# Gathers of a pairwise-product recommender kernel let go by a count of finished pieces

## The chip, the core and the metric

One core of one Trainium2 chip runs the whole program. The metric is the device time of one launch in microseconds. The five engines work in parallel: TensorE (PE in the rows; PEld is its weight load), VectorE (DVE), ScalarE (ACT), GpSimd (POOL) and SyncE (SP), ordered by semaphores that the kernel waits on.

## What is computed

A batch of 1024 rows looks up 32 embeddings of 64 numbers each in 32 tables. For each of the 496 pairs of fields (p, q) a 64x64 matrix multiplies one embedding and the result is multiplied with the other and summed; the 496 sums and 16 dense numbers go through three dense layers. All is float32.

```python
e = jnp.stack([tbl_0[ids[:, 0]], ..., tbl_31[ids[:, 31]]], axis=1)      # 1024 x 32 x 64
p = emb_inputs[:, ROW]
q = emb_inputs[:, COL]
kp = jnp.einsum('bpj,ipj->bpi', p, kernel)
outputs = jnp.sum(kp * q, axis=-1)                                       # 1024 x 496
...
h = jnp.concatenate([z, dense_ctx], axis=1)
h = jnp.maximum(h @ W_top1 + b_top1, 0.0)
h = jnp.maximum(h @ W_top2 + b_top2, 0.0)
y = h @ W_top3
```

## The kernel before

**Blocks and tiles.** The batch is cut into 4 blocks of 256 rows (`BLOCKS`, `SIZE`), the 32 fields into 16 tiles of two fields (`TILES`). Tile number m counts through all blocks: m = 16 b + tile (in block 0 the first five come in another order, `FRONT`). There are 64 (`LOOKED_UP`).

**Look-up of a tile (L369 to L383, GpSimd).** Four indirect gathers, one for each of two fields and two halves of 128 rows, each 128 rows of 64 numbers into `nat`, which has 8 places (`RING`); tiles 0 and 1 of a block go to `nat01`, which is doubled. They wait until tile m - 8 is transposed (L374), so that the place is free. Three tiles of block 0 (m = 0, 1, 3, `BY_PRODUCT`) are not gathered but looked up by a product with a one-hot matrix, so there are 61 look-ups, 244 gathers. The gathers of tile m count up `gathered[m % 8]`.

**Transposition.** TensorE transposes the gathered halves into `t_ps` (L586) and counts up `transposed`; ScalarE copies them to `rows` (L454) and counts up `rows_ready`. From block 1 on two tiles are transposed at a time.

**Pieces.** A piece is what VectorE multiplies in one instruction, 128x1024. There are two kinds. A *double* (48 a block) takes two pairs of tiles: TensorE multiplies `k_sb` with `rows` into one of three buffers of `u_ps` (L629, 8 matmuls; L636, 16 matmuls, for the two pieces of a block that pair the fields within tiles, multiplied by `by_self`), VectorE multiplies by `rows` (L549, or L552) into `prod`, and TensorE later adds up over the 64 partitions with `sel` into `z_ps` (L663, L669), four pieces behind. A *pass* (14 a block) has the batch on the partitions (L650, 8 matmuls), VectorE multiplies by `nat01` (L560), and ScalarE sums along the row with 16 pairs of small instructions (L466). So a block has 62 pieces, the kernel 248. TensorE may run three pieces ahead of VectorE (`URING`). Each product counts up `prod_ready`.

**Order.** A piece needs all tiles up to its own, so work opens up tile by tile: of a block, nothing but 7 pieces can be done without tiles 6 and up. `Plan` writes out one order of pieces for all engines by a small model of time: when a tile has landed (`landed`, with `issued`, `there`), it lets TensorE put its transposition behind every fourth double (`behind`) if it is there 1.5 us before, and before a piece (`before`) when nothing else is left. Every engine walks through that order.

**The sync queue (SP)** loads `k_sb` in 14 parts (the later ones behind `transposed`, L424), the swapped copies `by_self` (L411, behind `rows_ready`), and the weights of the towers.

**Ends.** Before the first piece TensorE and VectorE do the one-hot look-ups; behind the last piece come the three dense layers (L710, L730, L738).

Of the kernel before, what the change touches and what calls it, by code (L numbers as in the profile page):

```python
# [9 lines left out]
TILES = FIELDS // 2  # L10
# [3 lines left out]
SUBS = SIZE // P  # L14
# [18 lines left out]
ND = len(DOUBLES)  # L33
# [4 lines left out]
NP = len(IN_PASSES) // 2 * SUBS  # L38
# [35 lines left out]
URING, PRING, CRING, RING, LANES = 3, 8, 3, 8, 8  # L74
# [27 lines left out]
def tile_at(m):  # L102
    b, tile = divmod(m, TILES)
    return b, FRONT[tile] if b == 0 and tile < len(FRONT) else tile
# [11 lines left out]
def lane_count(m):  # L116

    return 32 * SUBS * (m // LANES + (m % LANES not in BY_PRODUCT))

K_FIRST = [min(d for d, double in enumerate(K_ORDER) if (double[1] or double)[0] == tile) for tile in range(2, TILES)] + [NK]
K_AFTER_TILE = [max(0, tile - 3) for tile in range(2, TILES)]

START, GATHER, LANDING = 3.2, 1.25, 2.35
PIECE, QUAD, TURN, TRANSPOSE, COPY, FOLD, FILL, PRODUCT, COMPARE = 0.87, 0.87, 0.17, 0.33, 0.55, 0.5, 0.23, 3.5, 3.2


class Plan:
# [7 lines left out]
    def __init__(self):  # L137
        self.order, self.before, self.behind, self.quads, self.sums, self.folded = [], [], [], [], [], []
        self.fill = [0] * LOOKED_UP
        self.now, self.copied, self.issued, self.there, self.done, self.here = 5.6, 0, START, [], [], []  # L140
        self.open, self.passes, self.summed, self.folds, self.doubles = [], 0, [], 0, 0
        while self.doubles < BLOCKS * ND:
            self.step()
        while self.open:
            self.add_sums(SUMS, 0)

    def landed(self, m):
        while len(self.there) <= m:
            n = len(self.there)
            if n in BY_PRODUCT:  # L150
                self.there.append(0)
                continue
            self.issued = max(self.issued, self.done[n - RING] if n >= RING else 0) + 2 * SUBS * GATHER
            self.there.append(self.issued - GATHER + LANDING)
        return self.there[m]

# [46 lines left out]
    def append(self, what):  # L203
        self.order.append(what)
        self.before.append(self.here)
        self.here = []
        self.behind.append([])
        self.quads.append(range(0))
        self.sums.append([])
        self.folded.append(None)  # L210
        self.now += PIECE
        self.add_sums(6 if len(self.open) == CRING or self.doubles >= (BLOCKS - 1) * ND else 4, 2)

    def add_double(self):
# [48 lines left out]
def tower(nc, ids, first_ids, tables, kern, dense, w1, b1, w2, b2, w3, out):  # L263
    f32, f32r, u32 = mybir.dt.float32, mybir.dt.float32r, mybir.dt.uint32
    ALU, ACT = mybir.AluOpType, mybir.ActivationFunctionType
    with ExitStack() as ctx:
# [6 lines left out]
        def sem(name):  # L273
            return ctx.enter_context(nc.semaphore(name))
# [69 lines left out]
        u_ready, prod_ready, summed, z_out = sem("u_ready"), sem("prod_ready"), sem("summed"), sem("z_out")  # L344
# [6 lines left out]
        def nat_of(m, s):  # L351

            b, tile = tile_at(m)
            return nat01[:, b % 2, s, tile, :] if tile < 2 else nat[:, m % RING, s, :]
# [5 lines left out]
        @block.gpsimd  # L360
        def _(pool):
            nc.gpsimd.memset(ident[:], 0.0).then_inc(ident_zero, 1)
            pool.wait_ge(ident_zero, 1)
            nc.gpsimd.affine_select(out=ident[:], in_=ident[:], compare_op=ALU.not_equal, fill=1.0, base=0,
                                    pattern=[[-1, P]], channel_multiplier=1).then_inc(ident_ready, 1)
            nc.gpsimd.iota(row_number[:], [[1, CHUNKS]], base=0, channel_multiplier=CHUNKS,
                           allow_small_or_imprecise_dtypes=True).then_inc(row_number_ready, 1)
            pool.wait_ge(ids_in, 16)
            for m in range(LOOKED_UP):  # L369
                if m in BY_PRODUCT:  # L370
                    continue
                b, tile = tile_at(m)
                if m >= LANES:
                    pool.wait_ge(transposed, m - LANES + 1)  # L374
                if tile == 0 and b >= 2:
                    pool.wait_ge(prod_ready, AT[b - 2, None, NP - 1] + 1)
                for n in range(SUBS):
                    for h in range(2):
                        f = 2 * tile + h
                        col = (b * SUBS + n) * FIELDS + f  # L380
                        pool.indirect_dma_start(  # L381
                            nat_of(m, n)[:, h * EMBED:(h + 1) * EMBED], None, tables[f],
                            bass.IndirectOffsetOnAxis(ids_sb[:, col:col + 1], 0)).then_inc(gathered[m % LANES], 16)  # L383
            for m in range(LOOKED_UP - LANES, LOOKED_UP):
                pool.wait_ge(gathered[m % LANES], lane_count(m))

        @block.sync
        def _(sp):
# [27 lines left out]

            for n, (first, end) in enumerate(zip(K_FIRST, K_FIRST[1:])):
                if K_AFTER_TILE[n] == 8:
# [372 lines left out]
```

## Time and profile before

| | us |
|---|---|
| median of three runs | 652.63 (644.64 to 654.17) |
| the profiled execution | 646.57 |
| its span, first to last instruction | 644.8 |
| mean granted TensorE clock, share of full speed | 0.849 |

The rows further below come from that one profiled execution. Times in them are microseconds from the first instruction, unless marked ns. In the timeline, `[6.68 <-PE t_ps L586]` is the time the engine stood before the instruction and what ended it; "issue" is a stretch in which the profile shows nothing to wait for, and "remote" or "another core or an unknown queue" one whose releaser is not found in the records. L381 is line 381 of the kernel. Matmuls are pipelined and their ends are modelled.

### The profile page before, as it was taken

To read this page: it belongs to the slowest core of one execution; us is meant where nothing else is said; L and a number is where in the kernel's file an instruction comes from. 1 tells how busy PE (TensorE), PEld (TensorE's weight loads), DVE (VectorE), ACT (ScalarE), POOL (GpSimd) and SP (SyncE) were. 2 spreads that over 40 slices of the span, in tenths; PEclk is the share of its full clock that TensorE was granted. 3 is DMA by queue.
4 is the path that set the end of the run, shared out by engine and by line. 5 is a ranking of instruction groups with operands and counts; after the bars stand their busy time and mean duration, and the time that the engine had idled before them with its cause. 6 is when DMAs were issued, how large, how long until landed. Compare 5 with 4: busy or idle time off the path is not lost.

```text
span 644.8 us, 9939 instructions
## 1 busy us (share of the span) xinstructions
PE 468.8 (73%) x3421; PEld 279.5 (43%) x3421; DVE 300.5 (47%) x281; ACT 257.9 (40%) x1862; POOL 238.6 (37%) x251
## 2 busy tenths in 40 slices
PE   7602498878668597765956595576675699999998
PEld 4401345444345354333534353243443366566443
DVE  7010467754526454543542464343463378888000
ACT  2101466554333555233543252633342377840121
POOL 8777354545444443144444414444414400000000
PEclk9856699898787897678988877797777799999999
DMA  3612264020042000020002000020000010100000
GB/s 112 182 26 58 68 191 150 18 50 18 16 115 51 17 15 13 7 49 17 18 16 50 16 5 16 18 48 17 13 5 17 17 34 3 34 2 2 0 1 1
DMA packets 18264, 24.29 MB, mean 38 GB/s; under 512 B 6387, under 2 KB 11767, under 8 KB 17958
## 3 DMA queue, kind: packets, MB, share of 16 engines
q1 hardware_dynamic: 10406, 15.64, 8.4%
q0 software_dynamic: 7808, 8.01, 6.6%
q8 instruction: 28, 0.46, 0.3%
q14 instruction: 22, 0.18, 0.1%
HBM read 19.44 MB, written 0.00 MB: 30 GB/s over the span
## 4 chain that ended last, share of the span: by engine, by line
PE 59%; another core or an unknown queue 25%; DVE 7%; issue 5%; POOL 2%; DMA 1%; ACT 0%; DVEq 0%
PE u_ps L629 22%; PE u_ps L650 11%; PE z_ps L663 10%; DVE prod L549 5%; PE z_ps L669 4%; PE u_ps L710 4%; PE t_ps L586 3%; POOL nat L381 2%; PE u_ps L730 2%; DVE pass_prod L560 2%; PE u_ps L636 1%; DMA nat<-tbl,ids_sb 1%; DMA ids_sb<-ids 0%; PE u_ps L738 0%
## 5 line engine op out<-in xcount | busy, mean ns | idle before, releaser
L381 POOL DMA_INDIRECT nat<-tbl,ids_sb x244 | 237.5, 973 | 270.5 <-PE t_ps L586 190.1
L549 DVE TENSOR_TENSOR prod<-u_ps,rows 128x1024 f32<-128x1024 f32 x184 | 215.0, 1219 | 248.7 <-remote 155.7
L629 PE MATMUL u_ps<-rows,k_sb 64*128 64x256 f32 x1472 | 194.6, 404 | 71.7 <-DVE prod L549 47.4
L466 ACT ACTIVATE pass_prod<-pass_prod 128x64 f32<-128x64 f32 x896 | 214.7, 243 | 57.2 <-DVE pass_prod L560 42.2
L629 PEld LDWEIGHTS u_ps<-rows,k_sb 64*128 64x128 f32 x1472 | 143.6, 194 | 130.2 <-issue 62.0
L466 ACT ACTIVATION_READ_ACCUMULATOR pass_prod<-pass_prod 128x1 f32 x896 | 170.0, 190 | 12.8 <-issue 12.4
L650 PE MATMUL u_ps<-k_sb,rows 64*128 64x256 f32 x448 | 86.2, 522 | 78.0 <-DVE prod L549 46.4
L454 ACT ACTIVATE rows<-t_ps 128x512 f32<-128x512 f32 (+1 forms) x38 | 19.6, 517 | 199.7 <-PE t_ps L586 140.7
L650 PEld LDWEIGHTS u_ps<-k_sb,rows 64*128 64x128 f32 x448 | 55.1, 253 | 101.8 <-DVE prod L549 59.4
L560 DVE TENSOR_TENSOR pass_prod<-u_ps,nat 128x1024 f32<-128x1024 f32 x56 | 67.9, 1220 | 32.3 <-PE u_ps L650 17.0
L663 PE MATMUL z_ps<-prod,sel 128*32 128x512 f32 x512 | 71.6, 684 | 0.0
L669 PE MATMUL z_ps<-prod,sel 128*32 128x256 f32 x512 | 34.0, 390 | 1.9 <-issue 1.7
L663 PEld LDWEIGHTS z_ps<-prod,sel 128*32 128x32 f32 x512 | 15.0, 124 | 36.4 <-issue 27.2
L586 PE MATMUL t_ps<-ident,nat 128*128 128x128 f32 x122 | 26.2, 338 | 6.1 <-DMA nat<-tbl,ids_sb 5.1
L710 PE MATMUL u_ps<-zT,rows 128*128 128x512 f32 x64 | 27.7, 594 | 0.0
L586 PEld LDWEIGHTS t_ps<-ident,nat 128*128 128x128 f32 x122 | 15.8, 168 | 24.0 <-issue 17.9
L669 PEld LDWEIGHTS z_ps<-prod,sel 128*32 128x32 f32 x512 | 16.2, 112 | 16.6 <-issue 8.1
L636 PE MATMUL u_ps<-rows,k_sb 64*64 64x256 f32 x128 | 10.5, 453 | 13.5 <-DVE prod L549 7.3
L710 PEld LDWEIGHTS u_ps<-zT,rows 128*128 128x128 f32 x64 | 12.1, 190 | 15.2 <-issue 15.2
L552 DVE TENSOR_TENSOR prod<-u_ps,by_self 128x1024 f32<-128x1024 f32 x8 | 9.7, 1219 | 12.9 <-remote 9.3
L508 ACT ACTIVATE k_sb<-u_ps,b_sb 128x512 f32<-128x512 f32 x8 | 5.5, 687 | 22.4 <-PE u_ps L710 22.4
L730 PE MATMUL u_ps<-k_sb,rows 128*128 128x512 f32 x32 | 13.9, 592 | 0.0
(44 smaller groups left out, 67.5 us busy)
## 6 DMA issues: line engine op xcount, KB each, us to landing
by_self<-rows SPq DMA_DIRECT2D x32, 128.0 KB
nat<-tbl,ids_sb POOLq DMA_INDIRECT x244
k_sb<-kern SPq DMA_DIRECT2D x3, 768.0 KB
k_sb<-kern SPq DMA_DIRECT2D x2, 640.0 KB
k_sb<-kern SPq DMA_DIRECT2D x1, 1152.0 KB
k_sb<-kern SPq DMA_DIRECT2D x2, 512.0 KB
rows<-w SPq DMA_DIRECT2D x1, 1024.0 KB
rows<-tbl SPq DMA_DIRECT2D x4, 224.0 KB
```

The costliest lines, as they stand in the source:

```text
L381: pool.indirect_dma_start(nat_of(m, n)[:, h * EMBED:(h + 1) * EMBED], None, tables[f], bass.IndirectOffsetOnAxis(ids_sb[:, col:col + 1], 0 ...
L454: nc.scalar.activation(rows[:, tile:tile + count, cols_of(b)], t_ps[:, 0:count].rearrange("p t n c -> p t (n c)"), ACT.Copy).then_inc(rows ...
L466: op = nc.scalar.activation(of, of, ACT.Copy, accum_out=z_nat[:, b % 2, s, row:row + 1])
L549: nc.vector.tensor_tensor(to, u, by.unsqueeze(1).to_broadcast([P, 2, 2, SIZE]), ALU.mult).then_inc(prod_ready, 1)
L560: nc.vector.tensor_tensor(pass_prod[:, k % CRING], u, by.to_broadcast([P, 2, 2, SIZE]), ALU.mult).then_inc(prod_ready, 1)
L586: op = nc.tensor.transpose(t_ps[:, t, s, :], nat_of(m + t, s), ident[:])
L629: op = nc.tensor.matmul(u[:, h, :], k_sb[part, k_of(d), side, :], rows[part, tile, cols_of(b)], start=True, stop=True)
L650: op = nc.tensor.matmul(u_ps[:, n % URING, h, t, :], rows[part, first + t, at:at + P], k_sb[part, k].rearrange("p s n -> p (s n)"), start= ...
L663: op = nc.tensor.matmul(z_ps[32 * k:32 * k + 32, :, :], sel[:, 30 - 2 * slot:62 - 2 * slot], prod[:, (a + k // 2) % PRING, k % 2], start=s ...
L669: op = nc.tensor.matmul(z_ps[32 * k:32 * k + 32, 0, :], sel[:, 30 - row:62 - row], prod[:, (a + k // 2) % PRING, k % 2, side], start=slot ...
L710: op = nc.tensor.matmul(h_ps(n), w1_sb[:, r * (HID1 // P) + m, :], zT[:, r, cols], start=r == 0, stop=r == ZROWS - 1)
L730: op = nc.tensor.matmul(h_ps(8 + n), w2_sb[:, g * (HID2 // P) + m, :], h1T(g, cols), start=g == 0, stop=g == HID1 // P - 1)
```

## The change

Before its four gathers, the look-up of tile m now also waits on `prod_ready` for `pieces_in_front(m, 0)`, which is floor(4 (m - 7) * 62 / 64), and zero up to m = 7. `AHEAD` is 7 tiles. The planner gets the same condition: `through[n]` is its time at which n pieces are multiplied, and a tile is not issued before `through[pieces_in_front(n, 0)]`. By this the order that it writes out can change, since a transposition is placed where its tile has landed. The rest of the program is the same text.

```diff
--- before.py
+++ after.py
@@ -119,6 +119,15 @@
 
 
 
+AHEAD = 7
+
+
+def pieces_in_front(m, part):
+
+    return max(0, (4 * (m - AHEAD) + part) * (ND + NP) // (4 * TILES))
+
+
+
 K_FIRST = [min(d for d, double in enumerate(K_ORDER) if (double[1] or double)[0] == tile) for tile in range(2, TILES)] + [NK]
 K_AFTER_TILE = [max(0, tile - 3) for tile in range(2, TILES)]
 
@@ -138,7 +147,7 @@
         self.order, self.before, self.behind, self.quads, self.sums, self.folded = [], [], [], [], [], []
         self.fill = [0] * LOOKED_UP
         self.now, self.copied, self.issued, self.there, self.done, self.here = 5.6, 0, START, [], [], []
-        self.open, self.passes, self.summed, self.folds, self.doubles = [], 0, [], 0, 0
+        self.open, self.passes, self.summed, self.folds, self.doubles, self.through = [], 0, [], 0, 0, [0]
         while self.doubles < BLOCKS * ND:
             self.step()
         while self.open:
@@ -150,7 +159,7 @@
             if n in BY_PRODUCT:
                 self.there.append(0)
                 continue
-            self.issued = max(self.issued, self.done[n - RING] if n >= RING else 0) + 2 * SUBS * GATHER
+            self.issued = max(self.issued, self.done[n - RING] if n >= RING else 0, self.through[pieces_in_front(n, 0)]) + 2 * SUBS * GATHER
             self.there.append(self.issued - GATHER + LANDING)
         return self.there[m]
 
@@ -209,6 +218,7 @@
         self.sums.append([])
         self.folded.append(None)
         self.now += PIECE
+        self.through.append(self.now + PIECE)
         self.add_sums(6 if len(self.open) == CRING or self.doubles >= (BLOCKS - 1) * ND else 4, 2)
 
     def add_double(self):
@@ -372,6 +382,8 @@
                 b, tile = tile_at(m)
                 if m >= LANES:
                     pool.wait_ge(transposed, m - LANES + 1)
+                if pieces_in_front(m, 0):
+                    pool.wait_ge(prod_ready, pieces_in_front(m, 0))
                 if tile == 0 and b >= 2:
                     pool.wait_ge(prod_ready, AT[b - 2, None, NP - 1] + 1)
                 for n in range(SUBS):
```

## Rows read from the trace of the kernel before

**Rows 1.** The page: its first line, busy time of the engines, and the chain by engine.
```profile
span 644.8 us, 9939 instructions
...
PE 468.8 (73%) x3421; PEld 279.5 (43%) x3421; DVE 300.5 (47%) x281; ACT 257.9 (40%) x1862; POOL 238.6 (37%) x251
...
PE 59%; another core or an unknown queue 25%; DVE 7%; issue 5%; POOL 2%; DMA 1%; ACT 0%; DVEq 0%
```

**Rows 2.** Costliest groups: line, engine, operation, count | busy, mean ns | idle before, releaser.
```profile
L381 POOL DMA_INDIRECT nat<-tbl,ids_sb x244 | 237.5, 973 | 270.5 <-PE t_ps L586 190.1
L549 DVE TENSOR_TENSOR prod<-u_ps,rows 128x1024 f32<-128x1024 f32 x184 | 215.0, 1219 | 248.7 <-remote 155.7
```

**Rows 3.** Timeline of GpSimd, 205 to 234 us: start, us, instruction, idle before.
```profile
210.62 0.94 POOL L381 DMA_INDIRECT nat<-tbl,ids_sb  x1 [6.68 <-PE t_ps L586]
...
219.35 0.94 POOL L381 DMA_INDIRECT nat<-tbl,ids_sb  x1 [0.30 <-issue]
```

**Rows 4.** Timeline of VectorE, 205 to 234 us.
```profile
210.74 1.22 DVE L560 TENSOR_TENSOR pass_prod<-u_ps,nat 128x1024 f32<-128x1024 f32 x1
221.31 1.22 DVE L552 TENSOR_TENSOR prod<-u_ps,by_self 128x1024 f32<-128x1024 f32 x1 [9.35 <-remote]
```

**Rows 5.** Timeline of TensorE, 205 to 234 us.
```profile
213.15 2.00 PE L629 MATMUL u_ps<-rows,k_sb 64*128 64x256 f32 x16
222.58 2.08 PE L629 MATMUL u_ps<-rows,k_sb 64*128 64x256 f32 x8 [7.43 <-DVE prod L552]
```

**Rows 6.** Timeline of GpSimd, 82 to 150 us.
```profile
84.49 0.94 POOL L381 DMA_INDIRECT nat<-tbl,ids_sb  x1 [1.86 <-PE t_ps L586]
...
136.84 0.94 POOL L381 DMA_INDIRECT nat<-tbl,ids_sb  x1 [4.50 <-PE t_ps L586]
...
140.59 0.94 POOL L381 DMA_INDIRECT nat<-tbl,ids_sb  x1 [0.30 <-issue]
```

**Rows 7.** Timeline of VectorE, 82 to 150 us.
```profile
88.77 1.23 DVE L549 TENSOR_TENSOR prod<-u_ps,rows 128x1024 f32<-128x1024 f32 x1 [1.47 <-PE u_ps L629]
...
142.59 4.62 DVE L549 TENSOR_TENSOR prod<-u_ps,rows 128x1024 f32<-128x1024 f32 x4 [4.19 <-PE u_ps L629]
```

**Rows 8.** Waits of VectorE, 182.13 to 500.26 us, then 84.49 to 148.09: total, times, longest.
```profile
DVE prod L549 <- remote: 104.2, 17, 11.3
...
DVE prod L549 <- PE u_ps L629: 17.1, 8, 4.2
```

**Rows 9.** Table of windows: us, busy (instructions) of each engine, TensorE clock, DMA share, GB/s.
```profile
84.49:148.09 63.60, 53.45 (x414) 31.27 (x410) 43.21 (x38) 36.38 (x289) 30.19 (x32) 0.95 0.31 88
182.13:500.26 318.13, 215.28 (x1548) 129.37 (x1544) 142.22 (x122) 127.38 (x944) 128.31 (x137) 0.80 0.13 27
533.20:597.73 64.53, 64.53 (x626) 40.97 (x621) 54.10 (x47) 32.95 (x261) 0.00 (x0) 1.00 0.04 10
597.73:644.80 47.07, 44.45 (x144) 19.29 (x136) 0.00 (x0) 9.01 (x14) 0.00 (x0) 1.00 0.00 1
```

**Rows 10.** Timeline of GpSimd, 0 to 120 us.
```profile
34.15 0.94 POOL L381 DMA_INDIRECT nat<-tbl,ids_sb  x1 [0.30 <-issue]
...
64.09 0.94 POOL L381 DMA_INDIRECT nat<-tbl,ids_sb  x1 [0.30 <-issue]
```

**Rows 11.** Chain that ended last, 0 to 80 us: start, us, what.
```profile
7.12 8.01 POOL nat L381
...
19.18 4.57 DMA nat<-tbl,ids_sb
...
27.19 7.92 another core or an unknown queue
...
36.36 10.70 another core or an unknown queue
...
48.31 23.28 another core or an unknown queue
```

**Rows 12.** Timeline of VectorE, 0 to 60 us.
```profile
11.76 3.25 DVE L538 TENSOR_SCALAR k_sb<-prod,row_number 125x512 f32<-125x512 f32 x8
```

## The prediction, written before the change was run

> **What bounds the kernel now.** I read the page first, then the chain of waits, then the timelines of VectorE, GpSimd and TensorE side by side. A *piece* below is one product of 128x1024 on VectorE with the TensorE matmuls that feed it; there are 248, 62 to a block. A *tile look-up* is four indirect gathers.
>
> The page shows no full engine. GpSimd is busy 37% of the span, and the chain that ended last gives 59% to TensorE and 25% to "another core or an unknown queue" [rows 1]. The cheapest-looking engine is the one to look at: the 244 gathers keep GpSimd busy 237.5 us, and VectorE's products, busy 215.0 us, stand idle 248.7 us before them, 155.7 us of it with no releaser named [rows 2]. This kernel has one core, so "remote" is not another core.
>
> The timeline of 205 to 234 us says what it is. GpSimd issues eight gathers in a row, the first at 210.62, the last at 219.35 (ends 220.29), and then stops [rows 3]. VectorE does a product at 210.74 and its next one at 221.31, after 9.35 us, 1.0 us behind the end of the last gather [rows 4]. TensorE had issued the last of the matmuls of three waiting pieces by 215.15, filled its three buffers and stood 7.43 us [rows 5]. So the matmuls went out, and the word that they were done came only when the run of gathers was over. The same is seen behind a run of four: its first gather starts at 136.84, its last at 140.59 (ends 141.53) [rows 6], and VectorE resumes at 142.59 after 4.19 us, again 1.0 us behind [rows 7]. In the waits of VectorE the stretch of single look-ups (84 to 148 us) holds no long wait without a releaser (17.1 us on L629, eight waits), the stretch of double ones 104.2 us in 17 waits [rows 8]: as many as the stretch has double look-ups.
>
> Stages, from the table of windows [rows 9]:
> - 533.2 to 597.73, no gather at all: 47 pieces in 64.53 us, **1.373 us a piece**, TensorE busy throughout. That is the work alone.
> - 84.49 to 148.09, eight look-ups one at a time (32 gathers): 38 pieces in 63.60 us. Work alone would take 52.2; 11.4 us are left, **1.43 us a look-up**.
> - 182.13 to 500.26, 34 look-ups two at a time (137 gathers): 122 pieces in 318.13 us against 167.5; 150.6 us are left, **4.43 us a look-up**.
>
> Why does half of a pair cost three times a single? TensorE can run three pieces ahead, about 3 us with the sums; a block of 4 us is mostly hidden, one of 10 us is not.
>
> The start is the worst of it. Behind the gather that ends at 15.13 [rows 11] GpSimd gathers without a pause to 65.03 [rows 10], and the chain has unnamed stretches of 7.92, 10.70 and 23.28 us there, ending at 71.59 [rows 11]. By 72.84 four pieces are done.
>
> A test of these prices on the kernel as it is: 72.84 + 244 x 1.373 + 10 singles x 1.43 + 40 of pairs x 4.43 = 599.4, measured 597.73.
>
> **The change, part by part.** The look-up of tile number m waits for floor(62 (m - 7) / 16) finished pieces: 3 for m = 8, 7 for m = 9, 217 for m = 63, so one look-up each 3.875 pieces. Nothing is removed, 56 waits are added, 61 look-ups stay. Queued behind each wait on GpSimd are only later look-ups. The sync queue's own waits stay where they were. The planner learns of the wait and puts the pairs of transposes later; their number stays.
>
> *Start.* Tiles 5, 6 and 7 are fetched as before, to 35.09 [rows 10]. Then GpSimd stops, since m = 8 wants three pieces. The second product runs from 35.14 to 36.36 as before. The third, whose matmuls are long issued, came after another 10.70 us, at 47.09, because gathers went on [rows 11]; now it needs only the release: it can start at 36.4, about 1.0 behind the last gather, and end at 37.6. The worst row is the release of 71.59, 6.6 us behind the last gather of that run [rows 10, 11], which gives 42.9. I take **38.0** for three pieces done, where it was 48.31, with 23.28 us more until the fourth could start.
>
> *The even middle, pieces 4 to 217.* 214 x 1.373 = **293.8 us** of work, and 56 look-ups, now single. Bound below: 1.43 us each, the mean of eight measured singles. Those had 7.95 us and 4.75 pieces to themselves, 2.2 us behind the release of VectorE 5.75 us after the first gather [rows 6, 7]; at 3.875 pieces and 1.43 us the period would be 6.75 and leave 1.0 us. Bound above, by hand: some 1.5 pieces get done before the block sets in, the release is 5.75 us after the first gather, and the 2.4 pieces still missing go at 1.15 us (four in 4.62 us [rows 7]); the period is 8.5 us, 3.2 us over the work. I take the middle, 2.3 us: **128.8 us** (80 to 179).
>
> *The end.* 31 pieces without look-ups: **42.6 us**; before, 47 pieces and more were free of gathers there [rows 9]. Towers and store, 597.73 to 644.8: **47.1 us**, unchanged, since TensorE does nothing else there [rows 9].
>
> *The new wait's own price.* The tightest place is tile 7 of a block: its look-up is let go at 62 b pieces, and pieces 62 b + 1 to 62 b + 7 are all that can be done without it. That is 7 x 1.94 = 13.6 us at the new pace, less three pieces by which TensorE runs ahead, 7.8 us. The four gathers start within 3.75 us, and the slowest landing the chain shows took 4.57 us [rows 11]: 8.3 us. Short by 0.5 us; with the copy behind it I put **3 us** for the three blocks. Where the cover fails, each of three tight pairs a block could cost some 3 us, 27 us in all.
>
> Sum: 38.0 + 293.8 + 128.8 + 42.6 + 47.1 + 3 = 553.3 of span, against 644.8. Around the span lie 1.8 us (646.57 for the profiled execution), so 555.1. The median before is 652.63, 6 us over the profiled one, with a spread from 644.64; I add nothing for it and say **555**.
>
> *A rule against it.* VectorE's products last 1.22 us inside a run of gathers and outside of it [rows 4, 7], while a gather beside the 125x512 comparisons of VectorE took 8.01 us instead of 0.94 and ended with them, at 15.1 [rows 11, 12]. The Trainium skill ("SBUF — State Buffer", SBUF: two separate sides) says that only VectorE and GpSimd share a port pair, as an exclusive lock taken by VectorE's two-port operations or those with two SBUF inputs, and that TensorE and ScalarE never wait on anyone. The long gather agrees. But by that rule gathers could not hold back TensorE's finished matmuls, the long waits would have another cause, and spacing the gathers would bring nothing; the rows of 1.0 us behind the last gather speak against it, and no row shows the mechanism.
>
> **The rivals.**
> - *Blocked only when crowded.* Look-ups with room around them cost nothing: 0 instead of 2.3 us, 553 - 129 = 424, up to 480 with part of it. For: behind the single that starts at 84.49 VectorE waits only 1.47 us, to 88.77 [rows 7]. Against: waits of 4.2 us behind singles [rows 7]. 9%.
> - *The price belongs to the later blocks, not to the pairing.* The tiles up to m = 23 cost 1.43 us, the 40 others 4.43: 38 + 293.8 + 22.9 + 177.2 + 42.6 + 47.1 = 621.6, with ends 600 to 638. For: no single look-up stands behind 148 us, so the two can't be told apart. Against: behind a single even VectorE waits no more than 4.19 us [rows 7], and three buffers cover part of that for TensorE. 14%.
> - *No effect.* The waits without a releaser come from elsewhere and merely fall together with gathers. Then pieces take as long as now, the span stays at 644.8, and the new waits add 3 to 27 us minus what little they hide: 640 to 660. The 17 waits for 17 doubles speak against it [rows 8]. 4%.
> - *Slower.* One mechanism: with a look-up each 3.875 pieces TensorE never rebuilds its lead, so every one of the 56 costs the 4.43 us of a pair's half, those of the first block too, which cost 1.43 now. 38 + 293.8 + 248.1 + 42.6 + 47.1 = 669.6. It decides from 4.0 us a look-up upwards. For: only 1.0 us of room between release and next gather. Against: the period of 7.95 us measured for singles [rows 9] was not much roomier. 5%.
>
> **How the numbers follow.** The likeliest, 68%, has its own range of 500 to 600 (1.43 to 3.2 us a look-up, with the start's and the wait's bounds). Reaching into the rivals until two in ten are left gives 482 to 625. Faster by over 2% (below 640) are the first case, the crowded one and the later-blocks one: 91%. Within 2%: 4%. Slower: 5%. About 2% is what a measurement of this kernel can tell from no change: its three runs lie 1.5% apart.
>
> **What would show it.** Right: unnamed waits of VectorE fall from 155.7 to under 60 us; no gap on VectorE over 6 us; GpSimd's runs are of four, the last one near 430 us instead of 510; four pieces done by about 40 us; TensorE's clock in the middle above the 0.80 of [rows 9]. Wrong in the main term: gaps of 4 to 5 us behind each run of four with TensorE idle in them. Wrong in the wait: transposes that wait for a gather's landing, at tiles 6 to 11 of a block. Wrong altogether: gaps that no longer follow the gathers.

## The result and the profile after

The changed kernel took 581.52 us (median of four, 579.21 to 584.44), the kernel before 653.4 us (median of four, 644.64 to 654.81): a ratio of 0.895 (0.887 to 0.903). The forecast was 555 us, with 500 to 600 us for its own case.

The page after: its first line, the chain by engine, and the two groups that answer to [rows 2].

```profile
span 582.5 us, 9993 instructions
...
PE 58%; another core or an unknown queue 21%; DVE 8%; issue 6%; ACT 5%; DMA 1%; POOL 1%; DVEq 0%; POOLq 0%; ACTq 0%
...
L393 POOL DMA_INDIRECT nat<-tbl,ids_sb x244 | 232.8, 954 | 264.4 <-DVE prod L561 140.2
L561 DVE TENSOR_TENSOR prod<-u_ps,rows 128x1024 f32<-128x1024 f32 x184 | 215.4, 1219 | 176.1 <-remote 92.0
```

GpSimd now stands mostly for VectorE's count (140.2 us of its 264.4), where it stood for a transposition before (190.1 of 270.5). VectorE's idle time before its products fell from 248.7 to 176.1 us, and the part without a releaser from 155.7 to 92.0.

The stages of the sum, from the table of windows after (columns as in [rows 9]; the first window runs from the third finished piece to the 217th):

```profile
39.11:493.60 454.49, 355.11 (x2728) 219.66 (x2724) 249.69 (x215) 223.85 (x1694) 208.09 (x220) 0.88 0.17 41
493.60:535.44 41.84, 41.79 (x413) 26.57 (x417) 35.62 (x31) 16.97 (x131) 3.79 (x4) 1.00 0.08 17
535.44:582.50 47.06, 44.45 (x144) 19.30 (x136) 0.00 (x0) 9.01 (x14) 0.00 (x0) 1.00 0.00 1
```

| stage | forecast | measured |
|---|---|---|
| to three pieces done | 38.0 | 39.1 |
| pieces 4 to 217, 56 look-ups | 422.6 | 454.5 |
| last 31 pieces | 42.6 | 41.8 |
| towers and store | 47.1 | 47.1 |
| waits for a landing | 3 | inside the second row |

The miss is in the second row: 160.7 us over the work in place of 128.8, **2.87 us a look-up** in place of 2.3. Not all of it is standing: in that row TensorE is idle for 99.4 us (454.49 less 355.11). The other 61.3 us are work that takes longer, 1.66 us of TensorE a piece (355.11 / 214) at a granted clock of 0.88, where the end of [rows 9] has 1.37 at 1.00.

Timeline of GpSimd after, 245 to 285 us: a look-up by itself, and two that ran together.

```profile
248.31 0.95 POOL L393 DMA_INDIRECT nat<-tbl,ids_sb  x1 [3.61 <-PE t_ps L598]
...
252.06 0.95 POOL L393 DMA_INDIRECT nat<-tbl,ids_sb  x1 [0.30 <-issue]
257.34 0.95 POOL L393 DMA_INDIRECT nat<-tbl,ids_sb  x1 [4.33 <-DVE prod L561]
...
265.11 0.95 POOL L393 DMA_INDIRECT nat<-tbl,ids_sb  x1 [3.06 <-DVE prod L561]
...
268.86 0.94 POOL L393 DMA_INDIRECT nat<-tbl,ids_sb  x1 [0.30 <-issue]
270.11 0.95 POOL L393 DMA_INDIRECT nat<-tbl,ids_sb  x1 [0.31 <-issue]
...
273.86 0.95 POOL L393 DMA_INDIRECT nat<-tbl,ids_sb  x1 [0.31 <-issue]
281.21 0.95 POOL L393 DMA_INDIRECT nat<-tbl,ids_sb  x1 [6.41 <-DVE prod L561]
```

Timeline of VectorE after, the same stretch:

```profile
254.21 4.63 DVE L561 TENSOR_TENSOR prod<-u_ps,rows 128x1024 f32<-128x1024 f32 x4 [4.41 <-remote]
...
267.64 1.22 DVE L572 TENSOR_TENSOR pass_prod<-u_ps,nat 128x1024 f32<-128x1024 f32 x1
275.81 4.63 DVE L561 TENSOR_TENSOR prod<-u_ps,rows 128x1024 f32<-128x1024 f32 x4 [6.95 <-remote]
```

A look-up alone still stops VectorE for 4.41 us here, till 1.2 us behind its last gather (252.06 + 0.95). Two run together when the count of the second is reached while the first is under way: the word of several finished pieces comes at once, VectorE does four in 4.63 us, and the next count (3.875 pieces on) is there. Then the stop lasts 6.95 us, till 1.0 us behind the last gather. From 75 us on there were 27 runs of four gathers and 10 of eight, and 12 gathers in shorter or broken runs.

The stops do not all end at one distance. From 39 us on VectorE stood over 3 us before a product 33 times: 17 of these stops ended 1.0 to 1.3 us behind the last gather of a run of four, 10 ended 1.0 to 2.3 us behind a run of eight, and 6 ended while a run still went on. So the end of a run is where most stops end, but the word can come earlier, as it did inside the first run of the kernel before [rows 11].

The start after, from the chain (start us, us, what):

```profile
17.78 14.37 another core or an unknown queue
...
44.60 6.54 issue
```

The first run is 20 gathers, to 29.74 us, and what the chain waited for came at 32.15, 2.4 us behind the whole of it; three pieces were done at 39.1. The second line lies under the next run, eight gathers from 39.88 to 49.58. GpSimd's timeline in the first run:

```profile
7.13 1.28 POOL L393 DMA_INDIRECT nat<-tbl,ids_sb  x1 [0.30 <-issue]
...
28.80 0.95 POOL L393 DMA_INDIRECT nat<-tbl,ids_sb  x1 [0.30 <-issue]
```

The gather that took 8.01 us in [rows 11], beside VectorE's comparisons, took 1.28 us here beside the same ones, as did the four after it, and so the run ended 5.3 us earlier than the forecast had it. The edit does not touch this place: in 11 of the 14 traces one gather stretches to 15.1 to 15.3 us (4.85 to 8.01 us long), in three, this one among them, none does (the other two have pauses there). These 5 us of the start are chance.

### The profile page after: what moved, and what is told of

Read it like the earlier page. It is cut to its first block, busy times and chain, and to the rows that moved or that the text cites. A ratio compares the mean times of both kernels' runs of the same rounds, so it can differ in the third digit from the quotient of the medians.

```text
span 582.5 us, 9993 instructions
## 1 busy us (share of the span) xinstructions
PE 464.6 (80%) x3421; PEld 281.4 (48%) x3421; DVE 300.4 (52%) x281; ACT 256.7 (44%) x1862; POOL 233.9 (40%) x251
## 3 DMA queue, kind: packets, MB, share of 16 engines
q0 software_dynamic: 7808, 8.01, 7.3%
## 4 chain that ended last, share of the span: by engine, by line
PE 58%; another core or an unknown queue 21%; DVE 8%; issue 6%; ACT 5%; DMA 1%; POOL 1%; DVEq 0%; POOLq 0%; ACTq 0%
PE u_ps L641 26%; PE u_ps L662 9%; DVE prod L561 7%; PE z_ps L675 7%; PE u_ps L722 5%; PE z_ps L681 4%; ACT pass_prod L478 4%; PE u_ps L742 2%; PE t_ps L598 2%; PE t_ps L617 1%; DMA nat<-tbl,ids_sb 1%; DVE pass_prod L572 1%; PE u_ps L648 1%; POOL nat L393 0%
## 5 line engine op out<-in xcount | busy, mean ns | idle before, releaser
L393 POOL DMA_INDIRECT nat<-tbl,ids_sb x244 | 232.8, 954 | 264.4 <-DVE prod L561 140.2
L561 DVE TENSOR_TENSOR prod<-u_ps,rows 128x1024 f32<-128x1024 f32 x184 | 215.4, 1219 | 176.1 <-remote 92.0
L641 PE MATMUL u_ps<-rows,k_sb 64*128 64x256 f32 x1472 | 216.0, 425 | 70.4 <-DVE prod L561 39.8
L641 PEld LDWEIGHTS u_ps<-rows,k_sb 64*128 64x128 f32 x1472 | 154.2, 206 | 138.5 <-issue 68.7
L662 PE MATMUL u_ps<-k_sb,rows 64*128 64x256 f32 x448 | 73.1, 452 | 27.2 <-ACT rows L466 13.8
L662 PEld LDWEIGHTS u_ps<-k_sb,rows 64*128 64x128 f32 x448 | 50.1, 225 | 45.2 <-issue 23.0
L675 PE MATMUL z_ps<-prod,sel 128*32 128x512 f32 x512 | 64.7, 625 | 0.0
L598 PE MATMUL t_ps<-ident,nat 128*128 128x128 f32 x122 | 23.6, 311 | 8.2 <-DMA nat<-tbl,ids_sb 4.3
L675 PEld LDWEIGHTS z_ps<-prod,sel 128*32 128x32 f32 x512 | 13.8, 113 | 30.6 <-issue 27.3
L598 PEld LDWEIGHTS t_ps<-ident,nat 128*128 128x128 f32 x122 | 14.0, 152 | 23.1 <-issue 23.1
L681 PEld LDWEIGHTS z_ps<-prod,sel 128*32 128x32 f32 x512 | 15.9, 116 | 14.7 <-issue 5.9
L491 ACT ACTIVATE zT<-t_ps 128x256 f32<-128x256 f32 x4 | 1.5, 385 | 38.9 <-remote 20.6
```

Of the source, the lines that this page charges most:

```text
L393: pool.indirect_dma_start(nat_of(m, n)[:, h * EMBED:(h + 1) * EMBED], None, tables[f], bass.IndirectOffsetOnAxis(ids_sb[:, col:col + 1], 0 ...
L561: nc.vector.tensor_tensor(to, u, by.unsqueeze(1).to_broadcast([P, 2, 2, SIZE]), ALU.mult).then_inc(prod_ready, 1)
L598: op = nc.tensor.transpose(t_ps[:, t, s, :], nat_of(m + t, s), ident[:])
L641: op = nc.tensor.matmul(u[:, h, :], k_sb[part, k_of(d), side, :], rows[part, tile, cols_of(b)], start=True, stop=True)
L662: op = nc.tensor.matmul(u_ps[:, n % URING, h, t, :], rows[part, first + t, at:at + P], k_sb[part, k].rearrange("p s n -> p (s n)"), start= ...
L675: op = nc.tensor.matmul(z_ps[32 * k:32 * k + 32, :, :], sel[:, 30 - 2 * slot:62 - 2 * slot], prod[:, (a + k // 2) % PRING, k % 2], start=s ...
```

## The experiments

The twelve kernels ran in three groups, each group on one chip together with the kernel before. That has to be said, since the kernel before itself took 639.54 us (635.76 to 648.2) in the first group, 636.9 us (633.79 to 642.79) in the second, and 418.51 us (414.53 to 419.96) in the third. Compare within a group, by the ratio; where a time is set beside one of another group, that is said. The kernels that leave out gathers or replace them (four of the twelve) were executed once each.

### First group: the wait, the order, the length of a run

**Only the planner's half.** The wait is taken out of the changed kernel:

```diff
-                if pieces_in_front(m, 0):
-                    pool.wait_ge(prod_ready, pieces_in_front(m, 0))
```

> Only the planner's half of the change: the order of pieces and transpositions of the changed kernel, no wait on the count of pieces. Theory (gathers in a run hold back TensorE's word that matmuls are done, and the wait spaces them): the start is as before, four pieces done at about 72 us, look-ups again two at a time behind a pair of transposes, 4.4 us lost to each; 640 to 665 us. Rival (the order written out by the planner brings the gain): 575 to 595 us.

Measured 628.01 us, ratio 0.983 (0.971 to 0.994) to before. Below the expected 640, but so was the kernel before in this group. The order alone brings 1.7% (0.6 to 2.9), not the 10.5% of the whole change. Timeline of GpSimd in it:

```profile
59.22 0.95 POOL L391 DMA_INDIRECT nat<-tbl,ids_sb  x1 [0.30 <-issue]
65.49 0.94 POOL L391 DMA_INDIRECT nat<-tbl,ids_sb  x1 [5.33 <-remote]
```

The run of the start goes on to 60.2 us as in [rows 10], four pieces are done only at 70.1, and 22 runs of eight are back.

**Two look-ups let go together.**

```diff
-                if pieces_in_front(m, 0):
-                    pool.wait_ge(prod_ready, pieces_in_front(m, 0))
+                if pieces_in_front(m | 1, 0):
+                    pool.wait_ge(prod_ready, pieces_in_front(m | 1, 0))
```

> The changed kernel, but both look-ups of a pair of tiles (2k, 2k+1) wait for the count of the second, so that eight gathers come in one run. Theory: the run's length sets the loss; 4.4 us a look-up as in the double ones of before in place of 2.9, so 56 x 1.5 = 84 us more, 650 to 680 us, if half of the runs had not been pairs already by themselves; with that 625 to 680. Rival (what counts is only how early a look-up comes, or how the start goes): within 10 us of the changed kernel's 582.

Measured 646.6 us, as the theory had it, ratio 1.012 (1.000 to 1.024) to before: the whole gain is gone, although the start keeps its gain (four pieces at 39.0) and all look-ups come by counts. Waits of VectorE in it (total, times, longest), against [rows 8] and 92.0 us in 20 waits in the changed kernel:

```profile
DVE prod L561 <- remote: 179.7, 37, 10.7
```

Not all of it is the longer run. The first look-up of each pair now also comes a look-up later, and TensorE stands more before its transpositions. The same wait in this kernel and in the changed one:

```profile
PE t_ps L598 <- issue: 29.1, 5, 6.4
```

```profile
PE t_ps L598 <- issue: 3.9, 3, 2.3
```

With the waits there that name a DMA (6.8 us for 4.3) that is 28 us, of the 55 us by which pieces 5 to 217 took longer than in the changed kernel (507.9 for 453.2). The rest fits longer runs, and this run alone does not part length from moment.

**A count for each gather.** Each of the four gathers waits for its own `pieces_in_front(m, part)`, with `AHEAD = 8`, and the planner is told the last:

```diff
-AHEAD = 7
+AHEAD = 8
...
                     for h in range(2):
+                        if pieces_in_front(m, 2 * n + h):
+                            pool.wait_ge(prod_ready, pieces_in_front(m, 2 * n + h))
```

> Each single gather waits for its own count, one gather for each piece (62 x 4 counts of 64), eight tiles ahead for the first and a little over seven for the last; the planner is told of the last one. Theory (the block sets in only behind the second gather in a row, so a lone gather costs little): under 1 us a look-up, middle stage 454 - 110 = 345 us, total 465 to 510 us. Rival A (each gather costs its share wherever it is, 0.7 us): 575 to 590. Rival B (each lone gather blocks until 1.0 us behind its end, so four blocks a look-up instead of one): 600 or more.

Measured 524.48 us, ratio 0.821 (0.814 to 0.828). Better than the changed kernel and 14 us above the theory's range, because the counts do not keep the gathers apart. Timelines of GpSimd and then of VectorE in it, 89 to 102 us:

```profile
90.00 0.95 POOL L393 DMA_INDIRECT nat<-tbl,ids_sb  x1 [2.72 <-DVE prod L561]
...
97.77 0.95 POOL L393 DMA_INDIRECT nat<-tbl,ids_sb  x1 [0.30 <-issue]
101.61 0.94 POOL L393 DMA_INDIRECT nat<-tbl,ids_sb  x1 [2.89 <-DVE prod L561]
```

```profile
93.04 2.35 DVE L572 TENSOR_TENSOR pass_prod<-u_ps,nat 128x1024 f32<-128x1024 f32 x2
100.12 2.36 DVE L561 TENSOR_TENSOR prod<-u_ps,rows 128x1024 f32<-128x1024 f32 x2 [4.73 <-remote]
```

VectorE works off six held pieces at 1.15 us each (four from 88.51, two from 93.04), faster than a gather is issued (1.25 us), and so lets go seven gathers nearly in a row, behind which the next word comes. A wait on a count that comes in bunches makes bunches.

**The second half without gathers.** In blocks 2 and 3 GpSimd skips its gathers (`if b >= 2: continue`), and the transposes wait for the earlier counts, so half of the output is of other rows.

> The changed kernel without the gathers of blocks 2 and 3: their tiles keep the rows of blocks 0 and 1, so the second half of the output is of other rows. All transposes, pieces and waits stay. Theory (the loss is the gathers'): from 97 pieces done at 238 us on 1.373 us a piece, 207 us, and 47 us of towers, so about 492 us, and no unnamed wait of VectorE behind 240 us. Rival (the loss comes from transposes, the swapped copies or the sums on ScalarE and only falls together with gathers): 570 to 585 us.

Measured 491.77 us, the expected 492. That it agrees to the microsecond is luck: 97 pieces were done at 230.0 us where 238 had been put, and the other 151 took 212.8 us for 207. Window from the 124th to the last piece:

```profile
267.80:442.70 174.90, 172.08 (x1624) 113.50 (x1620) 142.81 (x124) 115.28 (x891) 0.00 (x0) 0.99 0.06 14
```

124 pieces in 174.9 us, 1.41 us each, with all transposes, copies and sums in place; the changed kernel took 234.8 us for them (300.63 to 535.44 in the trace of the result). The loss belongs to the gathers.

### Second group: what about a gather hurts

**Plain copies from GpSimd** in blocks 2 and 3:

```diff
+                        if b >= 2:
+                            pool.dma_start(nat_of(m, n)[:, h * EMBED:(h + 1) * EMBED], tables[f][0:P, :]).then_inc(gathered[m % LANES], 16)
+                            continue
```

> The changed kernel; in blocks 2 and 3 each indirect gather is a plain copy of the first 128 rows of the same table, same size, same queue, same waits, so half of the output is of other rows. If what holds TensorE's word back is that GpSimd writes the descriptors of a transfer, plain or indirect: blocks 2 and 3 take as long as in the changed kernel (235 us from 124 pieces to the last), 570 to 590 us. If it is the indirection: blocks 2 and 3 at about 1.41 us a piece as without gathers (175 us), about 520 us.

Measured 492.47 us, under the 520 put for harmless copies: they stand in from the 97th piece on, not the 124th, which that sum overlooked. Windows: this kernel from its 124th to its last piece, and its look-ups on GpSimd's timeline:

```profile
270.10:443.50 173.40, 170.57 (x1628) 112.36 (x1624) 142.81 (x125) 115.41 (x891) 53.02 (x100) 1.00 0.12 33
```

```profile
333.93 2.12 POOL L394 DMA_DIRECT2D nat<-tbl  x4 [3.26 <-DVE prod L564]
338.45 2.12 POOL L394 DMA_DIRECT2D nat<-tbl  x4 [2.40 <-DVE pass_prod L575]
```

The same bytes, queue and waits cost nothing, and TensorE's granted clock is 1.00 (the higher of its two levels all through), where the changed kernel had 0.93 over its last 124 pieces. But four such copies last 2.12 us, not the 4.7 us of four gathers, so either the indirection or the length of the run may be what matters.

**Plain copies from the sync engine**, in the same two blocks, interleaved with its own loads by their counts.

> As the run before, but the plain copies of blocks 2 and 3 are issued by the sync engine, in the order of their counts among its own loads, with the same waits. The bytes and the destinations are the same. Theory S (descriptors made by GpSimd are what hurts): no unnamed waits behind 240 us, 490 to 510 us. Theory D (the traffic of 128 small packets into the partitions hurts, whoever makes it): as the changed kernel, 570 to 590 us.

Measured 494.48 us:

```profile
272.30:445.70 173.40, 170.56 (x1628) 112.33 (x1624) 142.81 (x125) 115.42 (x891) 0.00 (x0) 1.00 0.15 33
```

To the hundredth the same 173.40 us. The traffic into the partitions does not hurt, whoever issues it: theory D is refuted. Theory S is not confirmed by that, since plain copies issued by GpSimd are as harmless.

**Pauses.** The kernel with a count for each gather, and before the first and the third gather of each look-up from tile 8 on:

```diff
+                        if m >= LANES and h == 0:
+                            for _ in range(2):
+                                nc.gpsimd.memset(idle[:], 0.0).then_inc(idled, 1)
+                                slept += 1
+                                pool.wait_ge(idled, slept)
```

> The kernel with a count for each gather, and from tile 8 on GpSimd writes a scratch of 128x240 twice, waiting for each, after every second gather, some 0.7 to 0.9 us, so that no more than two gathers follow each other at once. Theory (runs of one and two cost about nothing, runs of three and more 2 to 3 us): 480 to 510 us, against 524 of the kernel without the pauses; the 224 gathers then need some 370 of the 390 us. Rival (a pause as short as this does not end a run, or GpSimd becomes the limit): 530 to 560 us.

Measured 478.73 us, 1 us below the theory's range, ratio 0.751 (0.746 to 0.757), where the kernel without the pauses had 0.821 in its group. GpSimd, and then VectorE, in it:

```profile
229.17 0.95 POOL L402 DMA_INDIRECT nat<-tbl,ids_sb  x1 [0.27 <-POOL idle L397]
230.42 0.95 POOL L402 DMA_INDIRECT nat<-tbl,ids_sb  x1 [0.30 <-DVE prod L570]
231.37 0.67 POOL L397 MEMSET idle<- 128x240 f32 x2
232.31 0.95 POOL L402 DMA_INDIRECT nat<-tbl,ids_sb  x1 [0.27 <-POOL idle L397]
```

```profile
233.75 1.23 DVE L570 TENSOR_TENSOR prod<-u_ps,rows 128x1024 f32<-128x1024 f32 x1 [1.32 <-PE u_ps L650]
...
241.70 3.49 DVE L570 TENSOR_TENSOR prod<-u_ps,rows 128x1024 f32<-128x1024 f32 x3 [0.69 <-PE u_ps L650]
```

With 0.94 us of other work after each second gather no wait near 4 us is left in this stretch, and the only wait of VectorE marked "remote" lies in the start, 8.0 us before 34.50 us, where no pause stands yet. Later on it still stands up to 8.0 us, as at 219.43 us, for matmuls (L650) that come late because TensorE stood before a transposition (4.91 us at 214.17, marked "issue"). What limits now is GpSimd itself. Two gathers and a pause start 3.14 us apart, a look-up takes 6.28 us where its 3.875 pieces of work take 5.3; 56 x 6.28 = 352 us, measured 342.3 from the fourth piece to the 217th.

**One tile earlier.** `AHEAD = 8` in the changed kernel, nothing else.

> The changed kernel with AHEAD = 8 in place of 7, one wait for each look-up as in it. It tells what of the gain of the kernel with a count for each gather (524 us) comes from the gathers' own counts and what from starting one tile earlier. Theory (spacing alone): 575 to 590 us. Rival (the lead): 540 to 560 us.

Measured 587.26 us, ratio 0.922 (0.911 to 0.932). No gain from the lead (the changed kernel had 0.895 in the runs of the result); the unbroken run of the start grew from 20 gathers to 28, and four pieces were done at 49.2 us. Since the kernel with a count for each gather also has AHEAD = 8 (ratio 0.821 in its group, against 0.922 here), its gain is from the gathers' own counts.

The loss by length of run, worked out from the traces from 75 us on: the time from the first gather of a run to the first of the next, less 1.373 us for each product that ended in it (runs with under 1.4 us between starts are one run; mean of all; the price of the lower clock is in it; e3 is the kernel with a count for each gather, e7 the paused one).

```
kernel         gathers in a run   runs   us lost to a run   us to the next run   pieces in it
before, to 180 us          4         9        1.54                7.79               4.56
before, from 180 us        8        17        8.86               18.71               7.18
changed, to 180 us         4         7        3.51                8.80               3.86
changed, from 180 us       4        19        2.87                8.21               3.89
changed, from 180 us       8         8        5.35               16.16               7.88
in pairs, from 180 us      8        19        7.95               18.65               7.79
e3, from 180 us            1        15        0.54                2.01               1.07
e3, from 180 us            2        10        0.41                3.02               1.90
e3, from 180 us            3         5        2.17                6.29               3.00
e3, from 180 us            4         6        2.18                7.90               4.17
e3, from 180 us            5         4        1.67                8.19               4.75
e3, from 180 us            6         7        2.79               10.25               5.43
e7, from 180 us            2        64        0.54                3.16               1.91
```

One and two gathers cost about 0.5 us, three to six 1.5 to 3.5 us. A run of eight cost 5.35 us in the changed kernel, 2.7 a look-up and so no more than a run of four there; in the other two kernels it cost 8 to 9 us. The length of a run alone does not set the price above three.

### Third group: a chip on which no hold shows

In this group the kernel before took 418.51 us. No trace of it on this chip is kept. Where the difference lies is seen in the one trace here that has long runs of gathers, that of the last kernel below: they hold nothing back.

**The kernel before with pauses** before the first and third gather of each look-up from m = 4 on, no counts.

> The kernel before, without any count of pieces and with its own order; only the pause of the run before (scratch of 128x240 written twice, waited for) stands before the first and the third gather of each look-up from m = 4 on. Theory (all of the loss is runs longer than two; the moment of a look-up matters not): no unnamed wait over 4 us, 475 to 500 us. Rival (the counts are needed to keep look-ups from crowding behind a pair of transposes): 530 to 580 us.

Measured 489.44 us, inside the range that the theory gave, and no confirmation of it: the kernel before took 418.51 us here, so the pauses made it slower, ratio 1.169 (1.162 to 1.176). Where the time goes is in the waits:

```profile
PEld t_ps L595 <- issue: 59.4, 32, 5.8
PE t_ps L595 <- issue: 48.1, 15, 5.4
```

TensorE stands before its transposes, most likely for landings, since a look-up takes 6.28 us of GpSimd and its pieces 5.3 us; the profile names no releaser. Against the first two groups the run does not decide whether counts are needed beside pauses. That stays open.

**Counts and pauses from m = 4 on.**

> The kernel of counts and pauses (478.7 us), the pauses now from m = 4 on in place of m = 8. Theory: the run of 15 gathers in the start falls apart too, four pieces are done before 36 us where it was 44.9, and the total is 465 to 474 us. Rival (the start is held by the loads of the k matrices and the one-hot look-ups): 476 to 481 us.

Measured 475.24 us, between the two ranges, ratio 1.136 (1.129 to 1.143) to the kernel before here. Four pieces were done at 28.2 us, but the start is free on this chip anyway, so it doesn't tell what the pause did.

One comparison across the groups is worth making. But for where the pauses begin, this is the kernel of 478.73 us in the second group: 3.5 us apart, while the kernels before them were 218 us apart. With pauses after each second gather the kernel runs alike on both chips, so what sets them apart went with the long runs, as far as kernels bound by GpSimd can tell.

**One write in each pause.**

```diff
-                            for _ in range(2):
+                            for _ in range(1):
```

> The kernel of counts and pauses (478.7 us) with one write of the scratch in place of two, so that some 0.6 us instead of 0.94 lie between two pairs of gathers. If any gap besides the usual 0.30 us ends a run: 470 to 480 us, GpSimd a little less in the way. If the gap must be near 0.9 us: runs join up, 495 to 530 us.

Measured 437.91 us, below both ranges, ratio 1.047 (1.038 to 1.056). A pair of gathers takes 2.79 us, a look-up 5.6; most of the 37 us against the run before are GpSimd's shorter pauses (0.7 a look-up; the pauses also begin later, at m = 8). Whether so short a pause ends a hold was not shown, as there was none to end.

**Plain copies cut in two**, eight to a look-up, in blocks 2 and 3.

> The kernel with plain copies from GpSimd in blocks 2 and 3 (492.5 us), each copy cut in two of half the width, so that a look-up is a run of eight transfers and some 4.2 us of GpSimd in place of 2.1. Theory (it is how long GpSimd makes transfers without a break, indirect or not): 2 us or more lost to each of 32 look-ups, 550 to 580 us. Rival (only the indirect gather holds TensorE back): 490 to 500 us.

Measured 431.71 us, inside neither range, on a chip where both were off. It was to tell indirection from length of run, and can't, on a chip without the hold. What it does show is the hold's absence in its first half, which is the changed kernel unchanged. Timeline of GpSimd and then of VectorE in it, in the midst of a run of 44 gathers (15.49 to 70.29 us, no two over 1.5 us apart):

```profile
64.19 0.95 POOL L398 DMA_INDIRECT nat<-tbl,ids_sb  x1 [0.30 <-issue]
65.61 0.94 POOL L398 DMA_INDIRECT nat<-tbl,ids_sb  x1 [0.47 <-issue]
```

```profile
53.24 4.65 DVE L566 TENSOR_TENSOR prod<-u_ps,rows 128x1024 f32<-128x1024 f32 x4 [1.38 <-PE u_ps L646]
...
60.18 4.65 DVE L566 TENSOR_TENSOR prod<-u_ps,rows 128x1024 f32<-128x1024 f32 x4 [1.16 <-PE u_ps L646]
...
67.12 4.62 DVE L566 TENSOR_TENSOR prod<-u_ps,rows 128x1024 f32<-128x1024 f32 x4 [1.16 <-PE u_ps L646]
```

VectorE does five pieces, waits 1.2 to 1.4 us for TensorE's matmuls, does five more, with gathers going on all the while; the kernel before stood 9.35 us behind a run of eight [rows 4]. The windows of this kernel, from the fourth piece to the 124th, and to the last:

```profile
33.10:206.30 173.20, 167.41 (x1510) 109.71 (x1510) 138.51 (x122) 119.73 (x925) 121.97 (x154) 0.98 0.31 78
206.30:382.70 176.40, 172.22 (x1624) 113.52 (x1620) 143.07 (x124) 115.31 (x891) 105.33 (x200) 0.99 0.13 32
```

The changed kernel was not run on this chip. An estimate from these rows: its first half is this one, 124 pieces done at 206.3 us. The kernel before ended at 418.5; less 1.8 us around the span, 47.1 of towers and the 176.4 us of the second window, it had 124 pieces done at about 193 us. So where nothing is held the changed order and waits would rather cost some 13 us than bring any.

## Why the prediction held, and where it missed

**What bounds the kernel: right on the chips that show the hold.** Taking the gathers out of one half brought its 124 pieces to 1.41 us each, plain copies in their place to 1.40, and lengthening or breaking the runs moved the ratio to the kernel before from 1.012 to 0.751 with the same work. That the hold is not there on every chip is what neither the prediction nor any of its rivals had; only the third group showed it.

**Start: right in size, not in its path.** 39.1 us for 38.0. But the forecast let the first two products go as before (25.96 and 35.14 us) and the run end at 35.09; in fact the run ended at 29.74, for no reason of the change, the first product came only at 35.05, and then all came quickly. Two errors cancelled, which is luck.

**Middle: the term that was mis-sized.** The work, 1.373 us a piece, holds (1.35 in the last 31 pieces). The price of a look-up was 2.87 us, not 2.3. The forecast took the middle between the eight singles of before (1.43) and a bound made by hand (3.2: held until 5.75 us after the first gather, then 2.4 pieces at 1.15). The bound was the truer half: singles cost 2.9 to 3.5 us in the table above. The mistake was to read the 1.43 us of [rows 9] as the price of a gather run. It is the period that moved little, 7.8 us before and 8.2 to 8.8 after; before, 4.6 pieces went into it, since a transposition let the look-up go, and now 3.9 do. The sum also had no term for the clock: it priced the work at 1.373 us a piece, measured at 1.00, for a stage that ran at 0.88.

**Runs of four: wrong for two look-ups in five.** Ten runs of eight, 20 of 50 look-ups, came about from 75 us on, through counts reached in bunches. They are not what raised the price, since they cost 2.7 us a look-up. The gap of VectorE over 6 us that was to be gone is there (8.03 at most), and the waits without a releaser are 92.0 us, not under 60. The last gather comes at 498 us; the "near 430" of the text did not even agree with its own sum, which gives 460.

**The new wait's own price: right to call it small.** One wait of TensorE that names a landing before a transposition, 4.3 us, and 3.9 us in three more that name nothing, in place of 3 us. The forecast's pace of 1.94 us a piece should have been 1.97 by its own sum (422.6 / 214), which changes nothing.

**Clock: right.** 0.88 of the higher level in the middle, for 0.80 in [rows 9] and 0.83 over all of the middle before (72.84 to 533.20 us). With fewer stands it is higher still: 0.93 with a count for each gather, 0.96 with the pauses.

**The rivals.** *The price belongs to the later blocks* is refuted: singles cost 2.87 us from 180 us on and 3.51 before. *Blocked only when crowded* as well, for four gathers (2.9 us lost with 8.2 us to the next run). *Slower through a lead never rebuilt* did not come, but two thirds of its price did (2.87 of 4.43). *No effect* is refuted on the chips with the hold. Its rule, that TensorE never waits on anyone (the Trainium skill, "SBUF — State Buffer", SBUF: two separate sides), was put down as spoken against by the rows. The third group agrees with it: 44 gathers in a row, and no stop of VectorE over 1.6 us from 33 us to the end of the run. In the first two groups finished matmuls were told late, but no row shows that a port held them, so the rule is neither shown nor refuted there. The long gather that the prediction counted for it came in 11 of 14 traces and not in the changed kernel's.

## What to carry to other kernels

When an engine waits with nothing to release it, lay the timelines of all engines side by side: here most long stops ended 1.0 to 2.3 us behind the last of a run of indirect gathers, and that named the remedy, shorter runs. Gate such a run by something that is even in time, not by a counter that advances in bunches; a count for each gather gave 18% and the same with a pause after every second gather 25%, where the count for each look-up gave 10.5%. And time both kernels on more than one chip before keeping a cure for a stall whose mechanism no row shows: on one of three groups there was no stall, and the two kernels with full pauses were 14% and 17% slower than the kernel before.

## What the runs showed of the hardware

- On the chips of the first two groups and in the runs of the result, behind three or more indirect gathers in a row (128 rows of 256 bytes, 0.94 us each, 1.25 us apart) the word of finished matmuls came late: in most cases 1.0 to 1.3 us behind the last of four and 1.0 to 2.3 us behind the last of eight, in some already inside the run. In the middle VectorE stood up to 11.3 us for it, in the start of the kernel before 23.3 us. After two gathers and 0.94 us of other work it did not. Plain copies of the same size (0.53 us each on GpSimd) did not, nor did copies from the sync engine.
- On the chip of the third group no such hold showed in a run of 44, and the kernel before took 418.5 us in place of 637 to 653. Whether it is the chip or its state at that time, what differs, and by which path a gather holds TensorE's word, no run here shows. Whether a longer run of plain copies would be held is open too.
- With plain copies in place of the gathers 124 pieces took 173.40 us, with the copies from GpSimd as from the sync engine.
- VectorE's comparisons (125x512, 5.4 to 15.0 us) stretched one indirect gather beside them to between 4.85 and 8.01 us in 11 of 14 traces. In the changed kernel's, five gathers beside the same comparisons took 1.28 us each. What decides between the two no run shows.
